# Tiles of 127 edges in place of 128 in a graph layer that gathers its node rows by indirect DMA

## Chip, core and metric

One core of a Trainium2 chip runs the whole kernel. The metric is the device time of one execution in microseconds, lower is better. Data is float32, with a few bfloat16 tiles for biases.

## What is computed

A layer of a graph network with 12500 nodes of 128 features and 212500 edges, which are sorted by their destination node. Cut to what matters:

```python
def layer(x, src, dst, edge_weight, edge_attr, w1, b1, w2, b2, lin1, lin2, lin2_b, lin, lin_b):
    h   = maximum(layernorm(x), 0)                          # [12500, 128]
    xp  = h @ lin1                                          # [12500, 128]
    C   = 0.5 * (cos(edge_weight * pi / 10) + 1)            # [212500]
    ssp = lambda v: softplus(v) - log(2)
    W   = (ssp(edge_attr @ w1 + b1) @ w2 + b2) * C[:, None] # [212500, 128], edge_attr has 50 columns
    agg = segment_sum(xp[src] * W, dst, 12500)              # gather by src, sum by dst
    return x + ssp(agg @ lin2 + lin2_b) @ lin + lin_b
```

## The kernel before

First the nodes: they are normalised and multiplied by lin1, and the product xp is written to a scratch tensor in HBM (xp_scratch). This part takes the first 68 us of the profiled execution.

Then the edges, which are most of the kernel. TILE = 128 edges are a tile, one edge to a partition, and QT = 4 tiles are a quad, QE = 512 edges. There are NT = 1661 tiles (the last has 20 edges) in NQ = 416 quads. Every engine runs its own loop over the quads, and semaphores join them; the order is that of the code. For a quad q:

- GpSimd (POOL) issues four indirect gathers, L307. Each reads one column of the index table IX, 128 row numbers, one per partition, and fetches 128 rows of 512 bytes from xp_scratch into a quarter of a buffer XG. There are XG_N = 6 such buffers, so before quad q POOL waits until PE has used quad q - 6 (semaphore s_sc). Nothing else is in POOL's loop.
- SyncE (SP) loads the edge attributes, 50 rows, for four quads in one DMA (L263, buffers AT), three in turn.
- TensorE (PE) multiplies the attributes by w1 (L605, PX), DVE and ACT make the softplus of it (L491, L371, L373, L482, tiles TB), and PE multiplies that by w2 (L619, PW), on top of the bias b2 that a matmul with a row of ones puts there (L617).
- DVE makes for each tile the matrix OH, 128 edges by a window of WIN = 64 nodes, that has C where the edge ends on that node (L500). It waits for PW and for the quad's four gathers, and multiplies: XG = PW * XG (L509). It is a single instruction for a quad, over 512 columns.
- PE sums by destination: PA = XG^T OH, accumulated over the four tiles (L631), and DVE adds this to the columns of AG that begin at the quad's first destination (L517).

After every 17 quads or so a chunk of 512 nodes is complete, and its last two matmuls, its softplus and its store are put between the quads (done_by and starts give the step at which that happens). A repair path after the loop does tiles again whose destinations don't fit the window of 64; with these inputs no tile is that wide, in tiles of either size.

Of the kernel before, what the change touches and what calls it, by code (L numbers as in the profile page):

```python
# [6 lines left out]
EDGES = 212500  # L7
D = 128
NG = 50
TILE = 128  # L10
NT = -(-EDGES // TILE)
QT = 4
QE = QT * TILE
NQ = -(-NT // QT)
WIN = 64
WIDE = 512
# [30 lines left out]
def quad(q):  # L47

    t0 = q * QT
    n = min(QT, NT - t0)  # L50
    last = min(TILE, EDGES - (t0 + n - 1) * TILE)
    return t0, n, last


def gnn_kernel(nc, x, src_t, dst_t, dbase, ew_t, attr_t, w1, b1, w2, b2, lin1, lin2, lin2b, lin, linb, eye, win, due, out):
# [9 lines left out]
    with ctx:  # L65
# [223 lines left out]
        @block.gpsimd  # L289
        def _(e):  # L290
            e.memset(AG[:, 0:AG0], 0.0).then_inc(s_ag, 1)
            for c in range(NNC):
                if c in BATCHES:
                    e.wait_ge(s_nw, BATCHES.index(c) + 1)
                norm(e, c, range(Y_POOL), s_yp)
            e.memset(AG[:, AG0:], 0.0).then_inc(s_ag, 1)
            e.wait_ge(s_ix, 16)
            for i in range(XG_N):
                n = len(range(i, NNC, XG_N))
                e.wait_ge(s_xs[i], 16 * n + (16 if (NNC - 1) % XG_N == i and NODES % TILE else 0))  # L300
            for q in range(NQ):
                t0, n, last = quad(q)
                if q >= XG_N:
                    e.wait_ge(s_sc, q - XG_N + 1)
                for k in range(n):
                    p = last if k == n - 1 else TILE
                    e.indirect_dma_start(XG[q % XG_N][0:p, k * D:(k + 1) * D], None, xp,  # L307
                                         bass.IndirectOffsetOnAxis(ap=IX[0:p, t0 + k:t0 + k + 1], axis=0)
                                         ).then_inc(s_g[q % XG_N][k], 16)

        @block.scalar
        def _(e):
            def rstd(b):
                _, _, t0, t1 = batch(b)
                e.wait_ge(s_mv, b + 1)
                e.activation(RV[:, t0:t1], RV[:, t0:t1], ACT.Ln).then_inc(s_rl, 1)
                e.wait_ge(s_rl, b + 1)
                e.activation(RS[:, t0:t1], RV[:, t0:t1], ACT.Exp, scale=-0.5).then_inc(s_rs, 1)

            e.preload_act_table_set("natural_log_exp_and_others")  # L320
            def carry(c):

                n0, w, tiles = nodes(c)
                e.wait_ge(s_pp, c + 1)
                if c >= XG_N:
                    e.wait_ge(s_xs[c % XG_N], 16 * (c // XG_N))
                full = w // TILE * D
                ins = e.activation(XG[c % XG_N][:, 0:full], PN[c % 4][:, 0:full], ACT.Copy)
                if w % TILE:
                    m = w % TILE  # L330
                    ins = e.activation(XG[c % XG_N][0:m, full:full + D], PN[c % 4][0:m, full:full + D], ACT.Copy)
                ins.then_inc(s_xe, 1)

            def y_act(c):

                if c < NODES // 512:
                    if c in BATCHES:
                        e.wait_ge(s_nw, BATCHES.index(c) + 1)
                    if c >= 4:
                        e.wait_ge(s_ce, c - 3)  # L340
                    t = 4 * c + 3
                    e.activation(TB[c % 4][:, 3 * D:4 * D], X[:, t * D:(t + 1) * D], ACT.Relu,
                                 scale=RS[:, t:t + 1], bias=RV[:, t:t + 1]).then_inc(s_y, 1)

            rstd(0)
            y_act(0)
            for c in range(NNC + 1):
                for b in range(1, len(BATCHES) - 1):
                    if c == max(BATCHES[b] - 3, 1):
                        rstd(b)  # L350
                y_act(c + 1)
                if c < NNC:
                    n0, w, _ = nodes(c)
                    e.wait_ge(s_ce, c + 1)
                    if c >= 3:
                        e.wait_ge(s_pp, c - 2)
                    e.activation(ZT[c % 3][:, 0:w], PX[c % 3][:, 0:w], ACT.Relu).then_inc(s_re, 1)
                if 0 <= c - 1 < NNC:
                    carry(c - 1)
            e.wait_ge(s_cst, 1)  # L360
            e.wait_ge(s_cw, 1)
            e.activation(CK[:, :], CK[:, :], ACT.Sin, scale=float(np.pi)).then_inc(s_sin, 1)
            e.preload_act_table_set("natural_log_exp_and_others")
            for i in range(STEPS):
                q = i
                if q < NQ:
                    t0, n, last = quad(q)
                    w = (n - 1) * TILE + last
                    T = TB[q % TB_N]
                    e.wait_ge(s_cl, q + 1)  # L370
                    e.activation(T[:, 0:w], T[:, 0:w], ACT.Exp).then_inc(s_ex, 1)  # L371
                    e.wait_ge(s_ex, q + 1)
                    e.activation(T[:, 0:w], T[:, 0:w], ACT.Ln, scale=0.5, bias=HALF[:, :]).then_inc(s_ln, 1)  # L373
                if i - 1 in AT_STEP:
                    c = AT_STEP[i - 1]
                    n0, w, _ = nodes(c)
                    e.wait_ge(s_fc, c + 1)
                    e.activation(TF[:, 0:w], TF[:, 0:w], ACT.Exp).then_inc(s_fx, 1)  # L378
                    e.wait_ge(s_fx, c + 1)
                    e.activation(TF[:, 0:w], TF[:, 0:w], ACT.Ln, scale=0.5, bias=HALF[:, :]).then_inc(s_fl, 1)  # L380

        @block.vector
        def _(e):
# [87 lines left out]
                link(e.tensor_scalar(REL[:, nf * QT:NT], REL[:, nf * QT:NT], BF[:, nf:nf + 1], None, ALU.subtract))  # L471
            e.wait_ge(s_ag, 2)

            tail = EDGES - (NT - 1) * TILE
            for i in range(STEPS):
                q = i - 1
                if 0 <= q < NQ:
                    t0, n, last = quad(q)
                    w = (n - 1) * TILE + last
                    e.wait_ge(s_ln, q + 1)  # L480
                    T = TB[q % TB_N]
                    e.scalar_tensor_tensor(out=T[:, 0:w], in0=PX[q % X1_N][:, 0:w], scalar=B1[:, 1:2],  # L482
# [1 line left out]
                q = i  # L484
                if q < NQ:
                    t0, n, last = quad(q)
                    w = (n - 1) * TILE + last
                    e.wait_ge(s_x1, q + 1)
                    if q >= TB_N:
                        e.wait_ge(s_w, q - TB_N + 1)  # L490
# [3 lines left out]
                if 0 <= q < NQ:  # L494
# [1 line left out]
                    if q >= OH_N:  # L496
                        e.wait_ge(s_sc, q - OH_N + 1)
                    for k in range(n):
                        p = last if k == n - 1 else TILE
                        ins = e.tensor_scalar(OH[q % OH_N][0:p, k, :], WI[0:p, 0:WIN], REL[0:p, t0 + k:t0 + k + 1],  # L500
                                              CC[0:p, t0 + k:t0 + k + 1], ALU.is_equal, ALU.mult)
                    ins.then_inc(s_oh, 1)
                    e.wait_ge(s_w, q + 1)
                    for k in range(n):
                        e.wait_ge(s_g[q % XG_N][k], 16 * (q // XG_N + 1))
                    p = last if n == 1 else TILE
                    assert n == 1 or last == TILE
                    G = XG[q % XG_N][0:p, 0:n * D]
                    e.tensor_tensor(G, PW[q % 2][0:p, 0:n * D], G, ALU.mult).then_inc(s_m, 1)  # L509
                q = i - 5  # L510
                if 0 <= q < NQ:
                    e.wait_ge(s_sc, q + 1)
# [5 lines left out]
                if i == FLAG_STEP:  # L518

                    link(e.memset(CK[:, NT - 1:NT], 0.0))  # L520
                    for p, a, b in ((TILE, 0, NT - 1), (tail, NT - 1, NT)):
                        link(e.tensor_scalar(CK[0:p, a:b], REL[0:p, a:b], WIN - 0.5, None, ALU.is_gt))
                        link(e.scalar_tensor_tensor(out=CK[0:p, a:b], in0=REL[0:p, a:b], scalar=-0.5, in1=CK[0:p, a:b],
                                                    op0=ALU.is_lt, op1=ALU.add))
# [40 lines left out]
        def _(e):  # L565
# [27 lines left out]
            for i in range(STEPS):  # L593
                q = i
                if q < NQ:
                    t0, n, last = quad(q)
                    w = (n - 1) * TILE + last
                    k = q // CHQ
                    e.wait_ge(s_at[k % AT_N], 16 * (k // AT_N + 1))
                    if q < X1_N:  # L600
# [7 lines left out]
                if 0 <= q < NQ:  # L608
# [3 lines left out]
                        e.wait_ge(s_m, q - 1)  # L612
                    else:
                        e.wait_ge(s_xe, NNC)
                    p = last if n == 1 else TILE
                    P = PW[q % 2]
                    e.matmul(P[0:p, 0:n * D], ones[:, 0:p], BP[0][:, 0:n * D], start=True, stop=False)  # L617
                    for k in range(n):
                        ins = e.matmul(P[0:p, k * D:(k + 1) * D], TB[q % TB_N][:, k * TILE:k * TILE + p], W2[:, :],  # L619
                                       start=False, stop=(k == n - 1))  # L620
                    ins.then_inc(s_w, 1)
                q = i - 4
                if 0 <= q < NQ:
# [3 lines left out]
                    if q >= 2:  # L627
                        e.wait_ge(s_ac, q - 1)
                    for k in range(n):
                        p = last if k == n - 1 else TILE  # L630
                        ins = e.matmul(PA[q % 2][:, 0:WIN], XG[q % XG_N][0:p, k * D:(k + 1) * D],  # L631
                                       OH[q % OH_N][0:p, k, :], start=(k == 0), stop=(k == n - 1))
                    ins.then_inc(s_sc, 1)
                if 0 <= i - FLAG_STEP - 1 < NFL:
# [3 lines left out]
                        e.wait_ge(s_vb, 1)  # L638
                    else:
                        e.wait_ge(s_ft, j)  # L640
                    e.matmul(PF[0:1, 0:b - a], ones[:, 0:1], VB[:, a:b], start=True, stop=True).then_inc(s_fp, 1)
                if i - 3 in AT_STEP:
                    c = AT_STEP[i - 3]
                    n0, w, tiles = nodes(c)
# [12 lines left out]

        first.close()

        tail = EDGES - (NT - 1) * TILE  # L660

        flagged = nc.values_load(FL[0:1, 0:1], min_val=0, max_val=TILE)
        with nc.If(flagged > 0):
# [1 line left out]
            nc.all_engine_barrier()  # L665

            def fix(t, p):
                i = nc.sync.dma_start(AT[0][:, 0:p], attr_t[:, bass.ds(t * TILE, p)])
                i.then_inc(s_za, 16)
                nc.sync.wait_ge(s_za, 16)  # L670
                nc.sync.sem_clear(s_za)
# [39 lines left out]
            with nc.Fori(0, NT - 1) as t:  # L711
                found = nc.values_load(FT[0:1, bass.ds(t, 1)], min_val=0, max_val=TILE)
                with nc.If(found > 0):
                    fix(t, TILE)
            found = nc.values_load(FT[0:1, NT - 1:NT], min_val=0, max_val=TILE)
            with nc.If(found > 0):
                fix(NT - 1, tail)
# [92 lines left out]
```

## Time and profile before

| | us |
|---|---|
| device time, median of 3 runs | 2524.14 |
| lowest and highest of them | 2524.11, 2525.67 |
| span of the profiled execution, first to last instruction | 2162.6 |
| first gather starts in it | 68.0 |
| last gather starts in it | 2147.8 |

For the profiled execution the profile gives the span and no time beside it; the median is 361.5 us more than the span. How to read the profile: "busy" is the time in which an engine carries out instructions. PE is the matmuls of TensorE, PEld its weight loads, DVE VectorE, ACT ScalarE, POOL GpSimd. For a gather POOL's busy time is that of the preparation of the DMA and not that of the data's flight; "issue" is time in which an engine waited for nothing that the profile shows. "Releaser" is what ended an idle time. The DMA parts count packets, of all 16 DMA engines together.

### The profile page before, as it was taken

What the parts mean: (1) busy time and instruction counts of PE and PEld (TensorE: products, weight loads), DVE (VectorE), ACT (ScalarE), POOL (GpSimd) and SP (SyncE); (2) the same over time, 40 slices, a digit from 0 to 9 for tenths busy, and PEclk for the clock granted to TensorE, in tenths of its full rate; (3) what the DMA queues carried; (4) which work ended last, traced back from release to release, by engine and by line L of the source; (5) the groups of instructions that cost most, each with busy time, mean ns of one, the idle gap of its engine ahead of it and who ended that gap; (6) DMA issues with size and microseconds to landing.
All of it is one profiled execution on the core that took longest, in us unless ns stands there. A gap on an engine that the chain in (4) does not pass through costs nothing.

```text
span 2162.6 us, 28443 instructions
## 1 busy us (share of the span) xinstructions
PE 1804.4 (83%) x8534; PEld 1331.3 (62%) x8535; DVE 1433.5 (66%) x3688; ACT 636.2 (29%) x976; POOL 1626.7 (75%) x1742
## 2 busy tenths in 40 slices
PE   6888888888877888878888888888878888878887
PEld 6556666666655656656665666666656666655665
DVE  7867666666665666666666666666667666666665
ACT  6323232222222222222232222222322223222221
POOL 7877777777777777777777777777777777777775
PEclk9678787687787787887687877777778678788776
DMA  9322222222232222223232222222222222232221
GB/s 286 90 73 69 81 76 75 79 76 81 68 82 81 71 79 81 75 74 82 68 82 79 77 79 70 81 81 68 81 81 75 74 81 76 74 81 76 73 72 47
DMA packets 100170, 175.95 MB, mean 81 GB/s; under 512 B 29163, under 2 KB 67748, under 8 KB 94870
## 3 DMA queue, kind: packets, MB, share of 16 engines
q0 software_dynamic: 53152, 108.91, 18.0%
q1 hardware_dynamic: 46868, 65.22, 11.4%
q8 instruction: 72, 1.18, 0.2%
q14 instruction: 78, 0.64, 0.1%
HBM read 161.21 MB, written 12.80 MB: 80 GB/s over the span
## 4 chain that ended last, share of the span: by engine, by line
POOL 60%; issue 20%; PE 14%; DMA 3%; DVE 2%; DVEq 0%; ACT 0%; POOLq 0%; SPq 0%
POOL XG L307 59%; PE PW L619 4%; PE PA L631 4%; PE PX L605 3%; DMA XG<-xp_scratch,IX 3%; PE PW L617 1%; DVE SCR L403 1%; POOL TB L207 1%; DVE XG L509 1%; PE PF L648 0%; DVE MV L409 0%; PE PF L656 0%; PE PW L586 0%; DMA X<-x 0%; PE PX L573 0%
## 5 line engine op out<-in xcount | busy, mean ns | idle before, releaser
L307 POOL DMA_INDIRECT XG<-xp_scratch,IX x1661 | 1574.8, 948 | 507.4 <-issue 498.3
L371 ACT ACTIVATE TB<-TB 128x512 f32<-128x512 f32 x416 | 261.7, 629 | 1407.0 <-DVE TB L491 1406.9
L619 PEld LDWEIGHTS PW<-W,TB 128*128 128x128 f32 x3322 | 592.2, 251 | 21.4
L619 PE MATMUL PW<-W,TB 128*128 128x128 f32 x3322 | 594.5, 338 | 0.0
L509 DVE TENSOR_TENSOR XG<-PW,XG 128x512 f32<-128x512 f32 x416 | 286.2, 688 | 451.1 <-DMA XG<-xp_scratch,IX 448.1
L605 PE MATMUL PX<-AT,W 50*128 50x512 f32 x832 | 554.8, 752 | 7.1 <-DMA AT<-attr_t 7.1
L631 PEld LDWEIGHTS PA<-OH,XG 128*128 128x128 f32 x3322 | 544.4, 248 | 1.0 <-DVE XG L509 0.5
L631 PE MATMUL PA<-OH,XG 128*128 128x64 f32 x3322 | 543.3, 322 | 0.2 <-DVE AG L517 0.2
L617 PEld LDWEIGHTS PW<-BPB,ones 128*128 128x128 bf16 x416 | 41.3, 99 | 704.4 <-issue 649.6
L617 PE MATMUL PW<-BPB,ones 128*128 128x512 bf16 x416 | 195.2, 469 | 315.4 <-DVE XG L509 314.4
L491 DVE TENSOR_SCALAR TB<-PX,B 128x512 f32<-128x512 f32 x416 | 309.8, 745 | 202.9 <-PE PX L605 200.5
L500 DVE TENSOR_SCALAR OH<-WI,REL,CC 128x64 f32<-128x64 f32 x1661 | 427.3, 337 | 0.0
L482 DVE SCALAR_TENSOR_TENSOR TB<-PX,B,TB 128x512 f32<-128x512 f32 x416 | 309.2, 743 | 6.5 <-ACT TB L373 4.4
L373 ACT ACTIVATE TB<-TB,HALF 128x512 f32<-128x512 f32 x416 | 299.8, 721 | 13.5
L605 PEld LDWEIGHTS PX<-AT,W 50*128 50x128 f32 x832 | 142.2, 213 | 62.8 <-issue 32.0
L517 DVE TENSOR_TENSOR AG<-AG,PA 128x64 f32 x416 | 91.3, 219 | 46.3 <-issue 4.6
L207 POOL TENSOR_SCALAR TB<-X,RS,RV 128x128 f32<-128x128 f32 x74 | 40.9, 569 | 14.0 <-DVEq L425 9.4
L648 PE MATMUL PF<-L,TF 128*128 128x128 f32 x196 | 46.2, 365 | 0.0
L648 PEld LDWEIGHTS PF<-L,TF 128*128 128x128 f32 x196 | 38.6, 245 | 2.1
L378 ACT ACTIVATE TF<-TF 128x512 f32<-128x512 f32 (+1 forms) x25 | 15.5, 620 | 72.8 <-DVE TF L562 72.8
L573 PE MATMUL PX<-EYE,TB 128*128 128x128 f32 x98 | 17.6, 309 | 22.7 <-POOL TB L207 21.5
L656 PE MATMUL PF<-AG,L 128*128 128x512 f32 (+1 forms) x50 | 29.0, 665 | 1.5 <-DVE AG L517 1.5
(73 smaller groups left out, 329.2 us busy)
## 6 DMA issues: line engine op xcount, KB each, us to landing
AT<-attr_t SPq DMA_DIRECT2D x103, 400.0 KB
XG<-xp_scratch,IX POOLq DMA_INDIRECT x1661, 2.5
X<-x SPq DMA_DIRECT2D x12, 512.0 KB, 7.4
xp_scratch<-XG SPq DMA_DIRECT2D x24, 256.0 KB, 4.4
out<-X SPq DMA_DIRECT2D x24, 256.0 KB, 5.2
IX<-src_t SPq DMA_DIRECT2D x1, 830.5 KB, 6.5
CC<-ew_t SPq DMA_DIRECT2D x1, 830.5 KB, 8.4
DI<-dst_t SPq DMA_DIRECT2D x1, 830.5 KB
```

The source lines that it names most:

```text
L307: e.indirect_dma_start(XG[q % XG_N][0:p, k * D:(k + 1) * D], None, xp, bass.IndirectOffsetOnAxis(ap=IX[0:p, t0 + k:t0 + k + 1], axis=0)).t ...
L371: e.activation(T[:, 0:w], T[:, 0:w], ACT.Exp).then_inc(s_ex, 1)
L373: e.activation(T[:, 0:w], T[:, 0:w], ACT.Ln, scale=0.5, bias=HALF[:, :]).then_inc(s_ln, 1)
L482: e.scalar_tensor_tensor(out=T[:, 0:w], in0=PX[q % X1_N][:, 0:w], scalar=B1[:, 1:2], in1=T[:, 0:w], op0=ALU.add, op1=ALU.max).then_inc(s_h, 1)
L491: e.tensor_scalar(TB[q % TB_N][:, 0:w], PX[q % X1_N][:, 0:w], B1[:, 0:1], CLAMP, ALU.add, ALU.min).then_inc(s_cl, 1)
L500: ins = e.tensor_scalar(OH[q % OH_N][0:p, k, :], WI[0:p, 0:WIN], REL[0:p, t0 + k:t0 + k + 1], CC[0:p, t0 + k:t0 + k + 1], ALU.is_equal, AL ...
L509: e.tensor_tensor(G, PW[q % 2][0:p, 0:n * D], G, ALU.mult).then_inc(s_m, 1)
L517: e.tensor_tensor(A, A, PA[q % 2][:, 0:WIN], ALU.add).then_inc(s_ac, 1)
L605: e.matmul(PX[q % X1_N][:, 0:w], W1[:, :], AT[k % AT_N][:, o:o + w], start=True, stop=True).then_inc(s_x1, 1)
L617: e.matmul(P[0:p, 0:n * D], ones[:, 0:p], BP[0][:, 0:n * D], start=True, stop=False)
L619: ins = e.matmul(P[0:p, k * D:(k + 1) * D], TB[q % TB_N][:, k * TILE:k * TILE + p], W2[:, :], start=False, stop=(k == n - 1))
L631: ins = e.matmul(PA[q % 2][:, 0:WIN], XG[q % XG_N][0:p, k * D:(k + 1) * D], OH[q % OH_N][0:p, k, :], start=(k == 0), stop=(k == n - 1))
```

## The change

A tile becomes ET = 127 edges, and everything that follows from it: NT is 1674, the last tile has 29 edges, QE is 508, NQ is 419 and the last quad has two tiles. All buffers keep their size, with 128 partitions, of which the edge loop uses 127; the tables of indices, destinations and weights are laid out by the host in columns of 127 and one empty row. The last quad now has a full and a partial tile, so DVE's product and PE's L617 and L619 are split in two there.

```diff
 TILE = 128
-NT = -(-EDGES // TILE)
+ET = 127
+NT = -(-EDGES // ET)
 QT = 4
-QE = QT * TILE
+QE = QT * ET
...
                 for k in range(n):
-                    p = last if k == n - 1 else TILE
+                    p = last if k == n - 1 else ET
                     e.indirect_dma_start(XG[q % XG_N][0:p, k * D:(k + 1) * D], None, xp,
                                          bass.IndirectOffsetOnAxis(ap=IX[0:p, t0 + k:t0 + k + 1], axis=0)
                                          ).then_inc(s_g[q % XG_N][k], 16)
...
-                    w = (n - 1) * TILE + last
+                    w = (n - 1) * ET + last
...
-                    p = last if n == 1 else TILE
-                    assert n == 1 or last == TILE
-                    G = XG[q % XG_N][0:p, 0:n * D]
-                    e.tensor_tensor(G, PW[q % 2][0:p, 0:n * D], G, ALU.mult).then_inc(s_m, 1)
+                    whole = n if last == ET else n - 1
+                    if whole:
+                        G = XG[q % XG_N][0:ET, 0:whole * D]
+                        ins = e.tensor_tensor(G, PW[q % 2][0:ET, 0:whole * D], G, ALU.mult)
+                    if whole < n:
+                        G = XG[q % XG_N][0:last, whole * D:n * D]
+                        ins = e.tensor_tensor(G, PW[q % 2][0:last, whole * D:n * D], G, ALU.mult)
+                    ins.then_inc(s_m, 1)
...
     def tiles(a):
         a = _np.asarray(a)
-        a = _np.concatenate([a, _np.zeros(NT * TILE - EDGES, a.dtype)])
-        return _np.ascontiguousarray(a.reshape(NT, TILE).T)
+        a = _np.concatenate([a, _np.zeros(NT * ET - EDGES, a.dtype)]).reshape(NT, ET)
+        return _np.ascontiguousarray(_np.pad(a, ((0, 0), (0, TILE - ET))).T)
```

No instruction changes its place. What stands on POOL's queue from the memsets of AG to the end of the gathers, of before (TB is the normalised tile, x and a number is how often a row stands there):

```order
L291 MEMSET AG 128x6656
L207 ISA
L207 TENSOR_SCALAR TB<-X,RS,RV 128x128 x73
L207 TENSOR_SCALAR TB<-X,RS,RV 84x128
L296 MEMSET AG 128x6144
L307 DMA XG<-xp_scratch,IX 128x128 x1660
L307 DMA XG<-xp_scratch,IX 20x128
```

And of the changed kernel:

```order
L292 MEMSET AG 128x6656
L208 ISA
L208 TENSOR_SCALAR TB<-X,RS,RV 128x128 x73
L208 TENSOR_SCALAR TB<-X,RS,RV 84x128
L297 MEMSET AG 128x6144
L308 DMA XG<-xp_scratch,IX 127x128 x1673
L308 DMA XG<-xp_scratch,IX 29x128
```

The gathers stand where they stood, 13 more of them, and each has 127 rows.

## Rows read from the trace of the kernel before

**Rows 1.** The page, first line and part 1: busy time, share of the span, instructions.

```profile
span 2162.6 us, 28443 instructions
...
PE 1804.4 (83%) x8534; PEld 1331.3 (62%) x8535; DVE 1433.5 (66%) x3688; ACT 636.2 (29%) x976; POOL 1626.7 (75%) x1742
```

**Rows 2.** The page, part 4: the chain that ended last, by engine and by line.

```profile
POOL 60%; issue 20%; PE 14%; DMA 3%; DVE 2%; DVEq 0%; ACT 0%; POOLq 0%; SPq 0%
POOL XG L307 59%; PE PW L619 4%; PE PA L631 4%; PE PX L605 3%; DMA XG<-xp_scratch,IX 3%; PE PW L617 1%; DVE SCR L403 1%; POOL TB L207 1%; DVE XG L509 1%; PE PF L648 0%; DVE MV L409 0%; PE PF L656 0%; PE PW L586 0%; DMA X<-x 0%; PE PX L573 0%
```

**Rows 3.** The page, part 5: groups; busy us, mean ns of one | idle before, releaser.

```profile
L307 POOL DMA_INDIRECT XG<-xp_scratch,IX x1661 | 1574.8, 948 | 507.4 <-issue 498.3
...
L619 PE MATMUL PW<-W,TB 128*128 128x128 f32 x3322 | 594.5, 338 | 0.0
...
L605 PE MATMUL PX<-AT,W 50*128 50x512 f32 x832 | 554.8, 752 | 7.1 <-DMA AT<-attr_t 7.1
...
L631 PE MATMUL PA<-OH,XG 128*128 128x64 f32 x3322 | 543.3, 322 | 0.2 <-DVE AG L517 0.2
...
L617 PE MATMUL PW<-BPB,ones 128*128 128x512 bf16 x416 | 195.2, 469 | 315.4 <-DVE XG L509 314.4
```

**Rows 4.** Timeline of POOL (one of DVE), loop's start, mid-span: start, us, instruction [idle before <-releaser].

```profile
68.03 1.16 POOL L307 DMA_INDIRECT XG<-xp_scratch,IX  x1 [1.50 <-DMA xp_scratch<-XG]
...
68.16 1.89 DVE L461 TENSOR_TENSOR CK<-CK 128x1661 f32<-128x1661 f32 x1 [0.53 <-ACT CK L362]
...
71.53 1.74 POOL L307 DMA_INDIRECT XG<-xp_scratch,IX  x1 [0.30 <-issue]
...
1001.58 0.95 POOL L307 DMA_INDIRECT XG<-xp_scratch,IX  x1 [0.30 <-issue]
1002.84 0.94 POOL L307 DMA_INDIRECT XG<-xp_scratch,IX  x1 [0.30 <-issue]
```

**Rows 5.** Line L307 alone: duration in ns, least, median, most; issue to landing.

```profile
L307 POOL DMA_INDIRECT XG<-xp_scratch,IX x1661: 895/944/2315, 68.0 to 2147.8; - x185
...
DMA to landing us min/median/max: 2.1/2.5/8.0
```

**Rows 6.** Timeline, end of the loop: gathers of the last quads.

```profile
2142.84 0.94 POOL L307 DMA_INDIRECT XG<-xp_scratch,IX  x1 [0.30 <-issue]
...
2146.58 0.94 POOL L307 DMA_INDIRECT XG<-xp_scratch,IX  x1 [0.30 <-issue]
...
2147.83 0.90 POOL L307 DMA_INDIRECT XG<-xp_scratch,IX  x1 [0.30 <-PE PA L631]
```

**Rows 7.** DMA: a 128-row gather's packets, the 20-row gather's, the queue over the span.

```profile
DMA packets 32, 0.07 MB, mean 60 GB/s; under 512 B 16, under 2 KB 16, under 8 KB 32
...
q0 software_dynamic: 32, 0.07, 20.0%
...
DMA packets 32, 0.01 MB, mean 7 GB/s; under 512 B 22, under 2 KB 32, under 8 KB 32
...
q0 software_dynamic: 53152, 108.91, 18.0%
```

**Rows 8.** Timeline, end of the loop: DVE's product and PE's last use of gathered rows.

```profile
2149.15 0.69 DVE L509 TENSOR_TENSOR XG<-PW,XG 128x512 f32<-128x512 f32 x1 [2.34 <-DMA XG<-xp_scratch,IX]
...
2150.31 2.40 PEld L631 LDWEIGHTS PA<-OH,XG 128*128 128x128 f32 x10 [0.45 <-DVE XG L509]
2150.34 0.27 DVE L509 TENSOR_TENSOR XG<-PW,XG 20x128 f32<-20x128 f32 x1
```

**Rows 9.** Waits: engine, line <- what it waited for: us in total, times, longest.

```profile
DVE XG L509 <- DMA XG<-xp_scratch,IX: 448.1, 272, 4.9
...
POOL XG L307 <- PE PA L631: 7.6, 25, 0.3
```

**Rows 10.** Stretches of 5 us: busy time per engine, granted clock, DMA share, GB/s.

```profile
1005.00:1010.00 5.00, 5.00 (x18) 3.29 (x18) 3.20 (x8) 1.35 (x2) 3.78 (x5) 0.54 0.19 52
1010.00:1015.00 5.00, 4.56 (x25) 2.84 (x25) 3.23 (x9) 1.35 (x2) 3.78 (x5) 1.00 0.21 56
```

More of the change, by code:

```diff
@@ L50, in quad @@
     n = min(QT, NT - t0)
-    last = min(TILE, EDGES - (t0 + n - 1) * TILE)
+    last = min(ET, EDGES - (t0 + n - 1) * ET)
     return t0, n, last
@@ L472, in _ @@
             e.wait_ge(s_ag, 2)
-            tail = EDGES - (NT - 1) * TILE
+            tail = EDGES - (NT - 1) * ET
             for i in range(STEPS):
@@ L478, in _ @@
                     t0, n, last = quad(q)
-                    w = (n - 1) * TILE + last
+                    w = (n - 1) * ET + last
                     e.wait_ge(s_ln, q + 1)
@@ L486, in _ @@
                     t0, n, last = quad(q)
-                    w = (n - 1) * TILE + last
+                    w = (n - 1) * ET + last
                     e.wait_ge(s_x1, q + 1)
@@ L498, in _ @@
                     for k in range(n):
-                        p = last if k == n - 1 else TILE
+                        p = last if k == n - 1 else ET
                         ins = e.tensor_scalar(OH[q % OH_N][0:p, k, :], WI[0:p, 0:WIN], REL[0:p, t0 + k:t0 + k + 1],
@@ L520, in _ @@
                     link(e.memset(CK[:, NT - 1:NT], 0.0))
-                    for p, a, b in ((TILE, 0, NT - 1), (tail, NT - 1, NT)):
+                    for p, a, b in ((ET, 0, NT - 1), (tail, NT - 1, NT)):
                         link(e.tensor_scalar(CK[0:p, a:b], REL[0:p, a:b], WIN - 0.5, None, ALU.is_gt))
@@ L596, in _ @@
                     t0, n, last = quad(q)
-                    w = (n - 1) * TILE + last
+                    w = (n - 1) * ET + last
                     k = q // CHQ
@@ L614, in _ @@
                         e.wait_ge(s_xe, NNC)
-                    p = last if n == 1 else TILE
                     P = PW[q % 2]
[L617 to L620, printed above, removed]
+                    whole = n if last == ET else n - 1
+                    if whole:
+                        e.matmul(P[0:ET, 0:whole * D], ones[:, 0:ET], BP[0][:, 0:whole * D], start=True, stop=False)
+                        for k in range(whole):
+                            ins = e.matmul(P[0:ET, k * D:(k + 1) * D], TB[q % TB_N][:, k * ET:(k + 1) * ET], W2[:, :],
+                                           start=False, stop=(k == whole - 1))
+                    if whole < n:
+                        T = TB[q % TB_N][:, whole * ET:whole * ET + last]
+                        e.matmul(P[0:last, whole * D:n * D], ones[:, 0:last], BP[0][:, whole * D:n * D],
+                                 start=True, stop=False)
+                        ins = e.matmul(P[0:last, whole * D:n * D], T, W2[:, :], start=False, stop=True)
                     ins.then_inc(s_w, 1)
@@ L629, in _ @@
                     for k in range(n):
-                        p = last if k == n - 1 else TILE
+                        p = last if k == n - 1 else ET
                         ins = e.matmul(PA[q % 2][:, 0:WIN], XG[q % XG_N][0:p, k * D:(k + 1) * D],
@@ L640, in _ @@
                         e.wait_ge(s_ft, j)
-                    e.matmul(PF[0:1, 0:b - a], ones[:, 0:1], VB[:, a:b], start=True, stop=True).then_inc(s_fp, 1)
+                    e.matmul(PF[0:1, 0:b - a], ones[0:ET, 0:1], VB[0:ET, a:b], start=True, stop=True).then_inc(s_fp, 1)
                 if i - 3 in AT_STEP:
@@ L658, in gnn_kernel @@
         first.close()
-        tail = EDGES - (NT - 1) * TILE
+        tail = EDGES - (NT - 1) * ET
         flagged = nc.values_load(FL[0:1, 0:1], min_val=0, max_val=TILE)
@@ L667, in fix @@
             def fix(t, p):
-                i = nc.sync.dma_start(AT[0][:, 0:p], attr_t[:, bass.ds(t * TILE, p)])
+                i = nc.sync.dma_start(AT[0][:, 0:p], attr_t[:, bass.ds(t * ET, p)])
                 i.then_inc(s_za, 16)
@@ L713, in gnn_kernel @@
                 with nc.If(found > 0):
-                    fix(t, TILE)
+                    fix(t, ET)
             found = nc.values_load(FT[0:1, NT - 1:NT], min_val=0, max_val=TILE)
```

## The prediction

> **What bounds the kernel now.** I read the shares first, then the chain, then the stretches in which the second engine comes close. The chain that ended last runs for 60% through POOL and for another 20% through "issue", and by line 59% of it is the gather of L307 [rows 2]. POOL is busy 75% of the span, PE 83% [rows 1]: the engine with the larger share isn't the one that sets the pace. The timeline of POOL shows why. In the middle of the span one gather follows the other every 1.25 us, 0.94 to 0.95 us busy and 0.30 us of issue [rows 4], and this hardly ever breaks: of POOL's 507.4 us of idle time 498.3 are issue, and only 7.6 us, in 25 pieces, are put down to PE giving a buffer back [rows 3, 9]. The check: 68.03 us before the first gather, 1660 periods of 1.25 us, and the 14.8 us from the start of the last gather at 2147.83 [rows 6] to the end come to 2158 us, against a span of 2162.6; the rest is the first four gathers, which took 1.16 to 1.74 us [rows 4], and a few single ones. Downstream everything waits for the gathers: DVE's product L509 waited 448.1 us for them in 272 pieces [rows 9], and PE's L617 314.4 us for that product [rows 3].
>
> PE is the second bound, and near. Its four groups of the loop take (594.5 + 554.8 + 543.3 + 195.2) / 416 = 4.54 us per quad [rows 3] against 4 x 1.25 = 5.0 us of gathers; in a stretch at a granted clock of 0.54 it was busy 5.00 of 5.00 us, in the next, at 1.00, 4.56 [rows 10]. It catches up at the higher clock.
>
> **What the change does, part by part.**
> (1) More gathers: 212500 edges make 1674 tiles in place of 1661. Thirteen gathers at 1.25 us, all on the bounding engine: +16.3 us. Nothing hides them.
> (2) Quads: 419 in place of 416. On PE that is 3 x 4.54 = 14 us, on DVE (1433.5 us busy in all [rows 1]) some 10 us; both lie beside POOL's longer loop, and count only where PE is the bound. The moving side of L605 is 508 columns and not 512, under 1% less. The two extra matmuls and the extra DVE product of the last quad are one small step each (the 20-row product at the end of before takes 0.27 us [rows 8]).
> (3) Loads of edge attributes: 50 rows of 8128 bytes in place of 8192, 105 loads in place of 104. SP's queue is off the chain; PE waited 7.1 us for one load in the whole span [rows 3], and that stays.
> (4) How one gather is carried out. This decides the result, and before has only one gather of another size, the last, with 20 rows. It shows two things. First the packets: a 128-row gather is 32 packets, 16 of them data (0.07 MB, so 4 KB or 8 rows each) and 16 under 512 bytes; the 20-row gather is also 32, but 10 are data (1 KB or 2 rows each) and 22 are under 512 bytes, six of them fillers [rows 7]. Rows are dealt out in equal shares: 16 x 8 and 10 x 2. 127 has no equal share but 1 x 127. So I expect one DMA engine to carry all 127 rows. Second the time on POOL: 0.90 us against 0.94 [rows 6] (the view of the line gives 895 ns as the least and 944 as the median [rows 5]): 49 ns less for 2 rows per engine in place of 8, which is 8.2 ns for each row in a share.
>
> The first consequence is a longer flight. The 16 data packets took 20.0% of 16 engines in 1.1 us, so 0.22 us each [rows 7]; one after the other on one engine they take 3.5 us, 3.3 us more than in parallel. A gather landed after 2.5 us in the median [rows 5], and would land after 5.8. That is covered: the first gather of the last full quad started at 2142.84, DVE's product came at 2149.15 and PE's last use ended by 2152.7 [rows 6, 8], so a buffer is held for some 10 us, and six buffers make it free for 30. With 3.3 us more, and with an attribute load in the way once in a while, POOL still doesn't wait. Only the end of the kernel sees it, and there the last gather has 29 rows and overlaps: +2 us. If the cover were gone, each quad would pay up to 3.3 us.
>
> The second is the preparation on POOL, which nothing covers. What the 49 ns stand for the trace doesn't say; three readings are open. (a) They are paid for each row of the longest share, because the sixteen shares are written side by side: then 127 rows in one share are 119 steps more than 8, 119 x 8.2 = 0.97 us per gather. (b) They are paid per row in all: 108 rows for 49 ns, nothing for 127 against 128. (c) They are paid per engine served: 6 engines for 49 ns, and 15 engines less would save 122 ns. I take (a), since equal shares, filled up with fillers on the engines that get no rows, look like one loop run by all sixteen at once, which is as long as its share. The bound above: the first gathers ran beside DVE passes over 1661 columns and took up to 1.74 us, 1.85 times the usual [rows 4]; if the longer writing were stretched so by DVE's passes all the time, it would be 1.8 us per gather. The bound below is reading (c), a gain. 1673 x 0.97 = +1627 us.
>
> The sum by (a): 16 + 1627 + 2 = +1645 us. The span, 2162.6 us, would become about 3810. Outside the span lie 2524.1 - 2162.6 = 361.5 us (the page gives no time of its own for the profiled execution beside its span; the three runs lie within 1.6 us), which I leave as they are. 2524 + 1645 = 4170 us. By then POOL's period is 2.22 us and a quad 8.9 us, so PE with its 4.54 is far from the bound.
>
> The Trainium skill bears on both steps. Its page "DMA: Bandwidth & Descriptors", section "Why a DMA increments its semaphore by 16 and not by 1", says that the number of engines is the largest up to 16 that divides the slowest dimension, names 127 partitions with one engine, and adds that some direct copies from GpSimd get shares that are rounded up; by that rule the landing is late as above, and the 20 rows of rows 7 fit it and its exception alike. The same page, in the table "Where the ~2 µs actually goes", calls the descriptor generation small and says that many can be emitted before the cost shows; by that the sum would be 2543 us, the first rival.
>
> **The rivals.**
> - The preparation costs what it did. Reading (b): only the 13 gathers and the late end count, 2524 + 16 + 3 = 2543 us. For it: 0.94 us is mostly something that doesn't depend on the rows at all, and a loop over rows would do 127 as fast as 128. The same time, within 3 us, comes out if the change doesn't do what it says, because the shares are rounded up to 15 x 8 + 7: 2540 us. Against: the fillers.
> - All gathers on the same engine. If the one engine is always the same, the gathers queue up on it. The gather queue's packets took 18.0% of 16 engines' span [rows 7], 0.18 x 16 x 2162.6 / 1661 = 3.75 us per gather, over POOL's 2.22: 1674 x 3.75 + 83 + 361 = about 6720 us. For it: nothing in the trace tells where the engine numbers start. Against: it would be a poor choice when several are in flight.
> - The other side: faster. Reading (c): with one engine served the preparation falls by 122 ns, 1674 x 0.122 = 204 us, less the 16 us: down to 2336. Since PE needs 4.54 us per quad and a period of 1.13 gives 4.5, PE would take over and hold it at about 2350. It decides from a saving of 16.3 / 1674 = 10 ns per gather. Against it: the engines without rows still got a filler and a small packet each, 32 packets in all [rows 7], so serving them isn't left out.
> - A step of a long share is dearer than the one pair of gathers shows, and the preparation grows by over 1.95 us: over 5800 us.
>
> **How the numbers follow.** Reading (a) 0.55, with 4170 us (3900 to 5600 its own range); preparation unchanged 0.28, with 2540 to 2545; one and the same engine 0.08; dearer still 0.04; faster 0.05. The predicted time is that of the likeliest, 4170. The range has to reach the unchanged preparation below, 2535, and the stretched writing above, 2524 + 16 + 1674 x 1.8 = 5550; the usual gathers differ by some 4 ns among themselves, which moves the 49 ns by 8%, and so this end to 5800; it leaves out 0.17. A measurement of this kernel can tell about 0.2% from no change, 5 us. All cases but the fast one are over that by the 13 gathers alone; I leave 0.02 for same (13 gathers partly made good by a slightly cheaper one), 0.05 for faster, 0.93 for slower.
>
> **What would show it.** The gather's mean on POOL: 1.9 us by (a), 0.94 by (b), 0.82 by (c). The packets of a gather: 16 data packets still, but on one engine. The landing: 5.8 us from issue if one engine carries it, 2.5 if shares are rounded up. POOL's idle time: issue alone, or DMA and PE releases if the engine is one and the same. PE's share falls to some 50% by (a) and stays at 83% by (b). I am wrong if the gather's time on POOL doesn't move; then the 49 ns were no price of a longer share.

## The result and the profile after

The changed kernel takes 4863.4 us (median of 4 runs, 4862.5 to 4863.8). The kernel before, in the four runs on record beside these, took 2524.9 us; that is a ratio of 1.926 (1.924 to 1.929). In all 25 later runs beside the experiments the kernel before took 2163.0 to 2166.1 us, and beside 11 of them the changed one again took 4862.2 us: 2.247 times (2.244 to 2.250). The profiled span of before, 2162.6 us, belongs to the second figure. A span and a device time are only about 2 us apart, as for the changed kernel (4861.1 and 4863.0 us). Why four runs of before took 361 us more isn't known. Nothing below rests on them: it rests on the two traces and on the later runs.

The page of the changed kernel: first line, part 1, part 3's line of the gather queue (packets, MB, share of 16 engines), part 4 by engine, and the groups of the gather, of DVE's product and of DVE's matrix OH.

```profile
span 4861.1 us, 28646 instructions
...
PE 2523.3 (52%) x8596; PEld 1833.4 (38%) x8597; DVE 1640.2 (34%) x3714; ACT 636.9 (13%) x982; POOL 4317.7 (89%) x1755
...
q0 software_dynamic: 455136, 121.66, 15.7%
...
POOL 80%; issue 10%; DMA 6%; PE 3%; DVE 1%; ACT 0%; DVEq 0%; POOLq 0%; SPq 0%; ACTq 0%
...
L308 POOL DMA_INDIRECT XG<-xp_scratch,IX x1674 | 4265.7, 2548 | 511.2 <-issue 499.6
...
L510 DVE TENSOR_TENSOR XG<-PW,XG 127x512 f32<-127x512 f32 x419 | 289.5, 691 | 3091.1 <-DMA XG<-xp_scratch,IX 3091.1
...
L501 DVE TENSOR_SCALAR OH<-WI,REL,CC 127x64 f32<-127x64 f32 x1674 | 622.1, 784 | 0.0
```

The gather's own line, and two rows from the middle of POOL's timeline:

```profile
L308 POOL DMA_INDIRECT XG<-xp_scratch,IX x1674: 1236/2548/3579, 67.8 to 4842.3; - x186
...
DMA to landing us min/median/max: 4.7/7.6/9.6
```

```profile
2001.20 2.55 POOL L308 DMA_INDIRECT XG<-xp_scratch,IX  x1 [0.31 <-issue]
2004.05 2.55 POOL L308 DMA_INDIRECT XG<-xp_scratch,IX  x1 [0.30 <-issue]
```

The difference is all in one number. A gather's preparation takes POOL 2.55 us in place of 0.94 [rows 4, 5], the 0.30 us between two of them stay, so a gather follows the last after 2.85 us and not 1.25. 1.60 us x 1673 = 2677 us; with the 16 us for 13 more gathers and 4 for the end (18.8 us from the start of the last gather to the end of the span, against 14.8) that is 2697, and the spans differ by 2698.5. POOL's idle time hardly moved, 511.2 us against 507.4 [rows 3], and 499.6 of it is still "issue": POOL waits for almost nobody. PE fell from 83% to 52% of the span, and DVE now waits 3091 us for gathers, from 448 [rows 9].

The queue's line shows how the rows were shared out. 455136 packets are 272 per gather, against 32 [rows 7]. Sixteen packets of up to 8 rows each carry 127 rows; sixteen are the small ones, one for each engine, that a 128-row gather has too. The other 240 are 15 x 16: each of the fifteen engines without rows has to work off as many packets as the one that has them. The bytes agree: 1674 tiles hold 212500 rows of 512 bytes, 108.8 MB, and the queue moved 121.66. The 12.8 MB more are 1673 x 15 x 127 x 4 bytes = 12.75 MB: one filler of 4 bytes on each idle engine for each row on the busy one. The sizes in the trace's packet records say the same: 376470 packets of 32 bytes (8 fillers) and 25095 of 28 (7 fillers), which is 15 x 15 and 15 for each of the 1673 gathers, and 45 of 32 bytes for the last.

### The profile page after: what moved, and what is told of

It reads as the page before. It is cut to its first block, busy times and chain, and to the rows that moved or that the text cites. A ratio compares the mean times of both kernels' runs of the same rounds, so it can differ in the third digit from the quotient of the medians.

```text
span 4861.1 us, 28646 instructions
## 1 busy us (share of the span) xinstructions
PE 2523.3 (52%) x8596; PEld 1833.4 (38%) x8597; DVE 1640.2 (34%) x3714; ACT 636.9 (13%) x982; POOL 4317.7 (89%) x1755
## 3 DMA queue, kind: packets, MB, share of 16 engines
q0 software_dynamic: 455136, 121.66, 15.7%
## 4 chain that ended last, share of the span: by engine, by line
POOL 80%; issue 10%; DMA 6%; PE 3%; DVE 1%; ACT 0%; DVEq 0%; POOLq 0%; SPq 0%; ACTq 0%
POOL XG L308 79%; DMA XG<-xp_scratch,IX 6%; PE PW L625 1%; PE PA L642 1%; DVE XG L510 0%; PE PW L623 0%; POOL TB L208 0%; DVE SCR L404 0%; PE PW L591 0%; DVE MV L410 0%; DMA X<-x 0%; PE PF L659 0%; PE PX L578 0%; POOLq L669 0%; ACT XG L329 0%
## 5 line engine op out<-in xcount | busy, mean ns | idle before, releaser
L308 POOL DMA_INDIRECT XG<-xp_scratch,IX x1674 | 4265.7, 2548 | 511.2 <-issue 499.6
L625 PEld LDWEIGHTS PW<-W,TB 128*127 128x127 f32 x3346 | 815.8, 335 | 37.7
L625 PE MATMUL PW<-W,TB 128*127 128x128 f32 x3346 | 800.7, 420 | 0.0
L610 PE MATMUL PX<-AT,W 50*128 50x508 f32 x838 | 765.6, 1011 | 6.7 <-DMA AT<-attr_t 6.7
L642 PEld LDWEIGHTS PA<-OH,XG 127*128 127x128 f32 x3348 | 755.4, 330 | 8.9 <-DVE XG L510 8.4
L642 PE MATMUL PA<-OH,XG 127*128 127x64 f32 x3348 | 742.8, 402 | 8.2 <-DVE AG L522 8.2
L501 DVE TENSOR_SCALAR OH<-WI,REL,CC 127x64 f32<-127x64 f32 x1674 | 622.1, 784 | 0.0
L483 DVE SCALAR_TENSOR_TENSOR TB<-PX,B,TB 128x508 f32<-128x508 f32 x419 | 310.0, 740 | 6.7 <-ACT TB L374 4.3
L492 DVE TENSOR_SCALAR TB<-PX,B 128x508 f32<-128x508 f32 x419 | 308.7, 737 | 5.2 <-PE PX L610 5.2
L374 ACT ACTIVATE TB<-TB,HALF 128x508 f32<-128x508 f32 x419 | 300.4, 717 | 13.5
```

Of the source, the lines that this page charges most:

```text
L492: e.tensor_scalar(TB[q % TB_N][:, 0:w], PX[q % X1_N][:, 0:w], B1[:, 0:1], CLAMP, ALU.add, ALU.min).then_inc(s_cl, 1)
L610: e.matmul(PX[q % X1_N][:, 0:w], W1[:, :], AT[k % AT_N][:, o:o + w], start=True, stop=True).then_inc(s_x1, 1)
L625: ins = e.matmul(P[0:ET, k * D:(k + 1) * D], TB[q % TB_N][:, k * ET:(k + 1) * ET], W2[:, :], start=False, stop=(k == whole - 1))
```

## Experiments

All times are compared with the kernel before on the same chip, 2163.7 to 2164.9 us.

**Three gathers in four at 128 rows.** Meant as the undoing of the gather's size alone, with tiles of 127 edges everywhere else:

```diff
-                    p = last if k == n - 1 else ET
+                    p = last if k == n - 1 else TILE
```

> The changed kernel with one thing undone: tiles of 127 edges everywhere, but each gather fetches 128 rows (the last row of a column is node 0, which nothing uses). Theory A (the gather's preparation on POOL grows with the rows in one engine's share, and nothing else of the change matters): POOL's mean back to 0.94 us a gather, 32 packets a gather, time that of before plus 13 gathers of 1.25 to 1.47 us, 2540 to 2545 us. Rival R1 (127 partitions on PE and DVE, or unaligned tiles of 508 columns, slow the loop): stays well above 2600 us.

It took 2860.9 us, 1.322 times before (1.320 to 1.324). The edit did less than was meant: `last` is 127 in a full quad, so the fourth gather of each kept 127 rows. POOL's timeline shows both kinds next to each other:

```profile
1505.65 0.95 POOL L308 DMA_INDIRECT XG<-xp_scratch,IX  x1 [0.30 <-issue]
1506.90 0.94 POOL L308 DMA_INDIRECT XG<-xp_scratch,IX  x1 [0.30 <-issue]
1508.15 2.55 POOL L308 DMA_INDIRECT XG<-xp_scratch,IX  x1 [0.30 <-issue]
1511.01 0.96 POOL L308 DMA_INDIRECT XG<-xp_scratch,IX  x1 [0.30 <-issue]
```

As an accident it is a good experiment. Same queue, same neighbours, one row less, 1.6 us more, in 418 gathers (the last quad's second gather has 29 rows): 418 x 1.60 = 669 us, on the 2182 us of the next experiment, is 2851. The other 10 us are in the 1255 gathers of 128 rows: their mean is 957 ns here, against 949 there, and why isn't shown. The expected 2540 to 2545 us were missed because the edit wasn't the one meant, so this run alone doesn't decide on R1; the next one does.

**All gathers at 128 rows.**

```diff
-                    p = last if k == n - 1 else ET
+                    p = TILE
```

> As e1_g128, but with every gather at 128 rows: there the fourth gather of each quad had kept 127 (its mean of 1354 ns is 3 x 956 and 1 x 2548). Theory A: POOL 0.94 us, period 1.25 us, so 1674 gathers take 16 us more than the 1661 of before, and the last one is of full size: 2164 + 16 = 2180 us (2176 to 2190). Rival R1 (partitions, columns and alignment of the tiles cost something): over 2190 us. The same kernel also says what the 13 gathers cost by themselves.

2182.1 us, 1.0083 times before (1.0069 to 1.0098): 18 us more, where 16 were expected, and inside the 2176 to 2190 us. Its queue, its gathers and, for later, DVE's matrix OH:

```profile
q0 software_dynamic: 53568, 109.81, 19.6%
...
L308 POOL DMA_INDIRECT XG<-xp_scratch,IX x1674 | 1588.4, 949 | 511.2 <-issue 499.4
...
L501 DVE TENSOR_SCALAR OH<-WI,REL,CC 127x64 f32<-127x64 f32 x1674 | 424.7, 334 | 0.0
```

32 packets per gather again. Everything else of the change, 127 partitions, 508 columns, shifted tiles, 3 more quads, costs nothing that can be told from the 13 more gathers: R1 is out. One unused row per gather is worth 2680 us.

**Other numbers of rows.** The constant alone is changed; the example is for 125:

```diff
-ET = 127
+ET = 125
```

> Tiles of 125 edges in place of 127: 1700 gathers, whose rows share out as 5 engines by 25 rows. Theory A, with the 13.5 ns per row of a share that the two traces give between 8 and 127: preparation 0.94 + 17 x 0.0135 = 1.17 us, period 1.48 us, span 1700 x 1.48 + 85 = 2600 us. Rival R2 (any number of rows that isn't a multiple of 16 takes a slow way of its own, whatever the share): preparation 2.5 us as with 127, some 4900 us. Rival R3 (the cost goes by the engines left out, 1.6 us for 15 of them): 11 left out, preparation 2.1 us, span some 4200 us.

> Tiles of 118 edges: 1801 gathers, 2 engines by 59 rows. Theory A: preparation 0.94 + 51 x 0.0135 = 1.63 us, period 1.94 us, span 1801 x 1.94 + 85 = 3580 us. R2: preparation 2.5 us, 5200 us. R3: 14 engines left out, preparation 2.43 us, span some 5000 us.

> Tiles of 120 edges: 1771 gathers, 15 engines by 8 rows. Theory A (only the length of the share counts): POOL 0.94 us as for 16 by 8, period 1.25 us, span 1771 x 1.25 + 88 = 2302 us. Rival R5 (numbers that aren't a multiple of 16 carry a charge of their own, which in 25 and 59 rows was hidden in the fit): 1.05 us or more, over 2480 us.

> Tiles of 126 edges: 1687 gathers, 14 engines by 9 rows. From the line through 15 x 8 (983 ns), 5 x 25 (1209) and 1 x 127 (2548), which is 13.2 ns for each row of a share: 996 ns, period 1.30 us, 1687 x 1.305 + 84 = 2286 us. Rival R6 (the cost goes by the number of rows in all, 128 being a special case): close to the 2548 ns of 127 rows, 4900 us.

> Tiles of 124 edges: 1714 gathers, 4 engines by 31 rows. From the same line 983 + 23 x 13.2 = 1286 ns, period 1.59 us, 1714 x 1.595 + 84 = 2818 us, so more than the 2667 us of 125 rows in 5 shares, although 124 is a multiple of 4. Rival R7 (only primes are bad): about 1000 ns, 2320 us.

| edges per tile | engines x rows | packets per gather | POOL, median ns | gathers | us, median | expected us |
|---|---|---|---|---|---|---|
| 128 (before) | 16 x 8 | 32 | 944 | 1661 | 2164 | |
| 120 | 15 x 8 | 32 | 983 | 1771 | 2374.3 | 2302 |
| 126 | 14 x 9 | 48 | 996 | 1687 | 2286.1 | 2286 |
| 125 | 5 x 25 | 80 | 1209 | 1700 | 2666.5 | 2600 |
| 124 | 4 x 31 | 80 | 1290 | 1714 | 2826.9 | 2818 |
| 118 | 2 x 59 | 144 | 1640 | 1801 | 3597.3 | 3580 |
| 127 (changed) | 1 x 127 | 272 | 2548 | 1674 | 4862.2 | |

The gather groups and queues of these kernels, for 120, 126, 125, 124 and 118 edges in this order. The group's mean lies 3 to 5 ns over the median:

```profile
q0 software_dynamic: 56688, 108.97, 17.9%
...
L308 POOL DMA_INDIRECT XG<-xp_scratch,IX x1771 | 1749.5, 988 | 541.3 <-issue 532.1
```

```profile
q0 software_dynamic: 80960, 109.03, 18.7%
...
L308 POOL DMA_INDIRECT XG<-xp_scratch,IX x1687 | 1687.2, 1000 | 515.1 <-issue 503.7
```

```profile
q0 software_dynamic: 136000, 110.78, 17.7%
...
L308 POOL DMA_INDIRECT XG<-xp_scratch,IX x1700 | 2063.2, 1214 | 519.6 <-issue 511.5
```

```profile
q0 software_dynamic: 137072, 111.46, 17.4%
...
L308 POOL DMA_INDIRECT XG<-xp_scratch,IX x1714 | 2218.0, 1294 | 523.4 <-issue 515.7
```

```profile
q0 software_dynamic: 259248, 114.86, 16.7%
...
L308 POOL DMA_INDIRECT XG<-xp_scratch,IX x1801 | 2959.4, 1643 | 550.1 <-issue 534.9
```

Two things are to be read here. The packets per gather, the queue's count over the number of gathers, are 16 x (share / 8, rounded up, + 1) in every row: for 9 rows 16 x 3 = 48, for 59 rows 16 x 9 = 144. The share is the number of rows over its largest divisor up to 16, and all sixteen engines get a list of that length. The bytes give the number of engines without rows in each kernel: for 118 rows 1801 x 14 x 59 x 4 bytes are 5.95 MB of fillers, and the queue moved 5.95 MB more than before; for 124 rows (12 x 31 a gather) it is 2.55 MB. And POOL's time is a line in the share: from 983 ns at 8 rows to 2548 at 127, 13.2 ns a row, on which 25 rows would be 1207, 31 rows 1286 and 59 rows 1654. The last gather of before has 2 rows in a share and takes 895 [rows 5]; the line gives 904. R2 (anything but a multiple of 16 is slow in one and the same way) asked for 2.5 us at 25 rows, R3 (by the engines left out) for 2.1 us there, R6 (by the rows in all) for 2.5 us at 126, R7 (only primes) for 1.0 us at 124: all four are out. 126 rows, one less than 127, are 2576 us faster.

Of the full gathers only those of 128 rows lie off the line, 39 ns below it. That is the share of 8 on sixteen engines; 15 x 8 costs 983. R5 asked for a charge of over 100 ns on numbers that aren't a multiple of 16; there is one, of 39. The three forecasts that started from the 944 ns came out low by it: by 72 us for 120 rows (1771 x 39 ns = 69 us), by 66 us for 125, and by 17 us for 118, where their steeper slope of 13.5 ns a row made up for most of it. With the 120-row kernel's period of 1.29 us, 1771 x 1.29 + 85 = 2370 us, against 2374 measured.

Whether every multiple of 16 is 39 ns cheaper is open. There is one other gather on sixteen engines, the last of the 126-row kernel, with 64 rows (16 x 4). It is the least of its line, 912 ns, which is 18 ns below the line through the others; but the last gathers with 1, 10 and 11 shares lie between 24 below it and 1 above, so this one doesn't show the 39:

```profile
L308 POOL DMA_INDIRECT XG<-xp_scratch,IX x1687: 912/996/2394, 68.1 to 2267.9; - x188
```

**Half the bytes.** The changed kernel with rows of 256 bytes: half of what each product reads isn't fetched.

```diff
-                    e.indirect_dma_start(XG[q % XG_N][0:p, k * D:(k + 1) * D], None, xp,
+                    e.indirect_dma_start(XG[q % XG_N][0:p, k * D:k * D + D // 2], None,
+                                         xp.rearrange("n (h d) -> (n h) d", h=2),
```

> The changed kernel with rows of 256 bytes in place of 512 in each gather: it fetches half the data (half of each product's input is left as it lies), the number of rows, fillers and gathers is the same. Theory A (the preparation on POOL is the whole cost, the flight on one engine is hidden): POOL stays at 2.55 us, time 4855 to 4865 us, only the landing falls, from 7.6 us to some 6. Rival R4 (POOL is held up by the one engine that has to carry 127 rows, 3.5 us against a period of 2.85): POOL and the time fall by at least 10%, to 4350 us or less.

4861.9 us. The gather's line:

```profile
L308 POOL DMA_INDIRECT XG<-xp_scratch,IX x1674: 1240/2548/3578, 69.0 to 4843.9; - x186
...
DMA to landing us min/median/max: 3.2/6.0/10.9
```

POOL's median is 2548 ns to the nanosecond and the landing 1.6 us earlier. R4 asked for at least 10% less time, so it is out: POOL isn't held up by the flight, and the flight is hidden.

**The two kernels as they are.**

> The changed kernel again, beside before on this chip, since before took 2163.7 us in the last runs and 2524.9 in the first ones. If only before has two speeds: 4863 us, ratio 2.248. If the chip of the first runs was slower for both, and the changed kernel is faster here: 4150 us or so, ratio 1.926.

> The kernel before, unchanged, for the gap of 361 us between its device time and its profiled span, which the changed kernel doesn't have (2 us). If the profiled execution was a quicker one than the timed ones, a new profile shows a span near 2522 us and a gather period near 1.47 us. If the gap is work outside the span, the span is 2163 us again.

4862.2 us for the changed one, and for before 2164.8 us with a span of 2162.8 and the gathers of the first profile:

```profile
L307 POOL DMA_INDIRECT XG<-xp_scratch,IX x1661: 895/944/2317, 68.8 to 2148.0; - x185
```

The changed kernel took the same in both sets, and before didn't, as the first case of the one expectation had it. Of the two cases of the other neither came as written. The first profile showed the kernel's usual pace, and no work lies outside its span; it is the four runs of 2524 us that were longer than all later ones. They weren't met again, so what made them longer stays open.

## Why the prediction was right, and where it was off

The direction, the engine, the place and the kind of cost were as forecast, and 4863 us lies in the range of 2535 to 5800; the time forecast was 4170. That the range reached so far up is owed to a cover that has another reason than what happened, as said below, and that 4170 looks near is owed in part to the 361.5 us.

- *POOL's gathers set the pace, and thirteen more cost 16 us.* Right: 18 us in the kernel that has only them and the small rest.
- *One engine carries all 127 rows.* Right, with 16 data packets as forecast; the 240 packets of fillers weren't in the forecast. The equal shares were read from the 20-row gather, and hold for 120, 126, 125, 124 and 118. The rule of the Trainium skill on the number of engines, "DMA: Bandwidth & Descriptors", section "Why a DMA increments its semaphore by 16 and not by 1", holds in every row of the table; its exception for direct copies, with shares that are rounded up, doesn't reach to these gathers.
- *Not always the same engine.* Right, as far as times can tell; the trace doesn't name the engine. The data packets of the changed kernel took 5972 us by its packet records, 3.57 us a gather, and its span is 4861 us: one engine that works off one packet after the other can't have had them all. It would have held POOL up in the end, and landings would have grown; POOL waited for PE 11.6 us in all, and no landing took over 9.6 us.
- *The flight gets 3.3 us longer and is hidden.* Right. The landing, counted from the start of POOL's instruction, rose by 5.1 us, from 2.5 [rows 5] to 7.6. Of this 1.6 us are the longer preparation, and 3.5 are left for the flight. The forecast of 5.8 us had left its own longer preparation out. The half-size rows moved the landing without moving the time.
- *Reading (a): 8.2 ns for each row of a share.* The mechanism was right and the size wrong, and this is the step that failed. I drew a line through two gathers that aren't on one line: the 20-row gather (895 ns, share of 2) and the 128-row one (944 ns, share of 8), and the second has the 39 ns discount of 16 x 8. Against 983 ns, what a share of 8 costs otherwise, the same difference is 88 ns for 6 rows, 14.7 ns each; over the whole line it is 13.2. So the term was 119 x 13.5 = 1.60 us per gather (with the lost discount in it) and not 0.97: 2677 us and not 1627, 1050 us too few.
- *What lies around the span, 361.5 us.* This was wrong too, with the other sign: it was no part of the kernel that one could leave as it is, but came with four runs that didn't repeat. It hid a third of the first error. Span to span I forecast 2162.6 + 1645 = 3808 us, and it was 4861.
- *The bound from the DVE passes, 1.8 us per gather.* It was a cover for the range and happened to hold 1.60, but its reason wasn't what filled it: the 2548 ns are the same in nearly all gathers.
- *Descriptor generation is small*, the rule beside the first rival (the Trainium skill, "DMA: Bandwidth & Descriptors", the table "Where the ~2 µs actually goes"): this case's traces don't agree. The preparation is 2.55 of the 7.6 us from issue to landing with 127 rows, and 0.94 of 2.5 us already with 128, and the time of this kernel is set by it.

## What to carry to other kernels

Where indirect gathers set the pace, count a gather's cost by the longest share and not by its rows: the number of rows over its largest divisor up to 16. If that share is long, fetch unused rows up to a number with a short one; here a single unused row per gather, 128 in place of 127, saves 2680 of 4862 us. And before you draw a slope through two measurements, ask whether both take the same way: a point at the size that the code likes best isn't a point on the line for the others.

## What the runs showed of the hardware

- The preparation of an indirect gather on POOL takes 983 + 13.2 x (share - 8) ns for shares from 2 to 127 rows, within 24 ns (29 rows, the last gather of the changed kernel, 1236 ns against 1260 by the line), and 944 ns for sixteen shares of 8. The first gathers of each kernel, beside DVE's passes over all tiles [rows 4], take longer (up to 3579 ns in the changed one).
- Engines without rows aren't spared: each gets a list as long as the longest, 4 bytes an entry (272 packets and 7.6 kB of fillers a gather with 127 rows). Whether POOL's time goes by the length of one list or by the entries of all sixteen, these runs can't tell, since the two always went together.
- DVE pays for POOL's longer preparations, off the path. L501, which reads and writes SBUF, took 784 ns in the mean in place of the 334 ns that it took with gathers of 128 rows (e5_all128), and at most 2126 ns. By the trace's records all 1008 of the 1674 that took over 500 ns ended within 0.1 us after a gather's preparation had ended, and so did all 65 of that kind in e5_all128; of the 619 that took 400 ns or less in the changed kernel 49 did. So the long ones are held until POOL has finished its preparation; what holds them isn't shown. In the kernel with half rows, where POOL does just the same, the median is higher still, 1143 ns; why isn't shown.

The line L501 alone, duration in ns, least, median, most, in the changed kernel, in the one with all gathers at 128 rows, and in the one with half rows:

```profile
L501 DVE TENSOR_SCALAR OH<-WI,REL,CC x1674: 296/691/2126, 84.2 to 4846.1; 127x64 f32<-127x64 f32 x186
```

```profile
L501 DVE TENSOR_SCALAR OH<-WI,REL,CC x1674: 296/308/569, 84.1 to 2167.3; 127x64 f32<-127x64 f32 x186
```

```profile
L501 DVE TENSOR_SCALAR OH<-WI,REL,CC x1674: 295/1143/2125, 85.4 to 4845.7; 127x64 f32<-127x64 f32 x186
```

- The gather queue's share with half the bytes rose from 15.7% to 32.5% of the sixteen engines' time, with fewer packets:

```profile
q0 software_dynamic: 240960, 67.26, 32.5%
```

  Twice as many fillers go into a packet there, and the time is in those packets: the 175680 of 64 bytes took 109 ns each in the mean, where the 376470 of 32 bytes in the changed kernel took 15 ns. It costs this kernel nothing, and why isn't shown.
